# Expert tiles of a routed FFN: 28 tiles of 256 rows, then units of 128 rows, with the short chunk of the hidden dimension first

## The reference

```python
x = x + _L0_xattn_ref(_layernorm(x, axis=-1), ctx_1024, ctx_1024, w_proj, b_proj)
x = x + _L0_ffn_ref(_layernorm(x, axis=-1), Wg, W1, W2, W3)

def _L0_ffn_ref(x, Wg, W1, W2, W3):          # 8 experts, hidden 682
    gate_logits = jnp.einsum('bsd,ed->bse', x, Wg)
    top_v, top_i = jax.lax.top_k(gate_logits, 2)
    ...
    gating = jax.nn.softmax(sparse_logits, axis=-1)
    h1 = jnp.einsum('bsd,ehd->bseh', x, W1)
    h2 = jnp.einsum('bsd,ehd->bseh', x, W2)
    hidden = jax.nn.silu(h1) * h2
    expert_out = jnp.einsum('bseh,edh->bsed', hidden, W3)
    return jnp.einsum('bsed,bse->bsd', expert_out, gating)
```

## Time and profile before

| | us |
|---|---|
| median of 3 runs | 873.97 |
| lowest, highest | 872.97, 878.98 |
| the profiled execution, its own time | 874.99 |
| its span, first to last instruction | 873.1 |

### The profile page before, as it was taken

The page is one execution under the profiler, slowest core; times in us unless marked ns, Lnnn a source line. Parts: engine busy times, 40 slices in busy tenths (PEclk is TensorE's granted clock), DMA queues, the critical chain, the costliest instruction groups (busy, mean ns, idle before and its releaser), DMA issues.

```text
span 873.1 us, 20010 instructions
## 1 busy us (share of the span) xinstructions
PE 784.8 (90%) x6472; PEld 481.2 (55%) x6472; DVE 602.1 (69%) x1224; ACT 557.6 (64%) x970; POOL 439.6 (50%) x431
## 2 busy tenths in 40 slices
PE   0578898989989899897989899999999999999995
PEld 0112233333333333332326788888888888888884
DVE  4888888979888898899924557555555555555553
ACT  3369789888897988966884454444444444444442
POOL 4555435786777868675643665222224222222222
PEclk9999999999999999999999999999999999999998
DMA  8575756866659685674266699999997699383832
GB/s 184 179 191 167 202 124 225 188 217 157 189 209 188 215 170 190 182 161 169 106 195 225 190 252 299 293 308 271 267 261 160 161 250 255 57 251 49 250 41 25
DMA packets 105959, 167.57 MB, mean 192 GB/s; under 512 B 54688, under 2 KB 83232, under 8 KB 101280
## 3 DMA queue, kind: packets, MB, share of 16 engines
q1 hardware_dynamic: 92448, 148.76, 60.0%
q0 software_dynamic: 13440, 17.90, 10.6%
HBM read 119.75 MB, written 42.55 MB: 186 GB/s over the span
## 4 chain that ended last, share of the span: by engine, by line
PE 48%; ACT 2%; issue 1%; POOL 1%; DMA 0%; DVE 0%; POOLq 0%; ACTq 0%; DVEq 0%
PE ps L1376 10%; PE ps L1378 10%; PE ps L1380 10%; PE ps L1394 4%; PE ps L1396 4%; PE ps L1398 4%; PE ps L1299 2%; ACT probs L842 1%; PE ps L1403 1%; PE ps L1284 1%; POOL slots L474 1%; ACT z_n L847 1%; PE ps L1327 0%; PE ps L1338 0%; PE ps L1271 0%
## 5 line engine op out<-in xcount | busy, mean ns | idle before, releaser
L973 DVE TENSOR_REDUCE neg_max<-ps 128x2 f16<-128x1024 f32 x256 | 309.1, 1221 | 37.6 <-PE ps L1271 32.9
L842 ACT ACTIVATE probs<-ps 128x1024 f32<-128x1024 f32 x256 | 259.0, 1024 | 61.7 <-PE ps L1284 61.2
L769 POOL DMA_INDIRECT out<-y,aim x72 | 113.4, 1574 | 237.6 <-DVE y L1202 160.0
L1376 PE MATMUL ps<-zt,w 128*128 128x256 f16 x792 | 216.0, 273 | 1.4 <-issue 1.3
L1378 PE MATMUL ps<-zt,w 128*128 128x256 f16 x792 | 215.9, 273 | 0.0
L1380 PE MATMUL ps<-zt,w 128*128 128x256 f16 x792 | 215.9, 273 | 0.0
L876 ACT ACTIVATE silu<-ps 128x256 f32<-128x256 f32 x216 | 82.7, 383 | 183.4 <-PE ps L1380 173.8
L1183 DVE SCALAR_TENSOR_TENSOR hid<-ps,silu 128x256 f32<-128x256 f32 x216 | 91.7, 425 | 136.0 <-ACT silu L876 128.3
L1299 PE MATMUL ps<-probs,v_ext 128*32 128x512 f32 x1024 | 138.7, 613 | 5.3 <-ACT heads L910 4.4
L1271 PE MATMUL ps<-k_stack,q_stack 48*128 48x512 f16 x512 | 104.3, 406 | 35.4 <-ACT probs L842 17.8
L1284 PE MATMUL ps<-q_stack,k_stack 49*128 49x512 f16 x512 | 101.9, 396 | 7.3 <-DVE neg_max L973 7.1
(11 more groups left out here) (126 smaller groups left out, 908.0 us busy)
## 6 DMA issues: line engine op xcount, KB each, us to landing
w<-w_parts SPq DMA_DIRECT2D x36, 1408.0 KB
w<-w_parts SPq DMA_DIRECT2D x36, 768.0 KB
w_in<-in_w SPq DMA_DIRECT2D x16, 704.0 KB, 6.0
v_ext<-in_v SPq DMA_DIRECT2D x8, 1024.0 KB, 5.6
k_stack<-k SPq DMA_DIRECT2D x48, 128.0 KB, 5.3
q_stack<-qt SPq DMA_DIRECT2D x48, 128.0 KB, 5.0
w_in<-in_w SPq DMA_DIRECT2D x8, 768.0 KB, 5.0
w_parts<-w_hi SPq DMA_DIRECT2D x16, 352.0 KB, 2.3
```

What stands on the lines that cost most here:

```text
L769: nc.gpsimd.indirect_dma_start(out=out, out_offset=bass.IndirectOffsetOnAxis(ap=aim[frm][:, t, 0:1].bitcast(U32), axis=0), in_=y[frm][:, t ...
L842: nc.scalar.activation(probs[g % 2][:, j:j + 2, k, :], pair_banks[PLACE["exp", u] % 3], ACT.Exp, scale=0.25).then_inc(s_exp, 1)
L973: nc.vector.tensor_reduce(neg_max[b % 2][:, i, c:c + 3:2], pair_banks[PLACE["max", u] % 3], AX.X, ALU.max, negate=True).then_inc(s_red, 1)
L1376: nc.tensor.matmul(dst, w[:, kk, 1, cols], z16[:, kk, :], start=(kk == 0), stop=False)
```

## The change

The 8192 rows are cut otherwise: `FULL_TILES` = 28 tiles of 256 rows, which any routing can fill by more than half, then units of 128 rows, of which `FIRM_UNITS` - 28 = 8 always exist and up to 7 more are behind a comparison. The units are straight code (15 copies on each engine) where before there was a loop of two tiles and one copy. A unit loads 128 rows, its matmuls of the up phase have 128 columns, its down phase has 16 matmuls, its ACT and DVE instructions are 128 wide, and it has one add. In each tile and unit the tail becomes the first chunk of the up phase, and the last but one of the down phase. `table` now runs three times: for tiles 0 to 11, for 12 to 27, and for the units; the third pass runs on DVE in four steps behind each of the tiles 6 to 11. SP waits for the second table before tile 12 and reads the number of units before it issues the first unit's loads. The zero rows are 128 per expert. Core of the diff:

```diff
-FIRM_TILES = 2 * TOKENS // SLOTS
-FFN_TILES = FIRM_TILES + E - 1
+FULL_TILES = (2 * TOKENS - E * P) // SLOTS
+FIRM_UNITS = FULL_TILES + 2 * TOKENS // P - SUB * FULL_TILES
+FFN_UNITS = FULL_TILES + (2 * TOKENS + E * (P - 1)) // P - SUB * FULL_TILES
+CHUNKS = (FULL,) + tuple(range(FULL))
...
+def subs(least):
+    return SUB if least < FULL_TILES else 1
+def subs_ahead(k):
+    return k * SUB if not isinstance(k, int) or k <= FULL_TILES else k + FULL_TILES * (SUB - 1)
...
+def last_units(eng, total, *steps):
+    for k in range(FIRM_UNITS, FFN_UNITS):
+        with eng.If(total > k):
+            for step in steps:
+                step(k, k // 2, k % 2, k)
...
-                rows = z_dram[bass.ds(first, SLOTS), :]
-                sp.dma_start_transpose(zt16[par][:, :, :], rows[:, 0:W].bitcast(F16)).then_inc(f_z[par], 16)
+                n = subs(least)
+                rows = z_dram[bass.ds(first, n * P), :]
+                sp.dma_start_transpose(zt16[par][:, :, 0:n * P], rows[:, 0:W].bitcast(F16)).then_inc(f_z[par], 16)
...
-                    sp.dma_start(z_dram[bass.ds(first, SLOTS), :].rearrange("(s p) c -> p s c", p=P),
-                                 fill[:, :, :]).then_inc(f_pad, 16)
+                    sp.dma_start(z_dram[bass.ds(first, P), :], fill[:, 0, :]).then_inc(f_pad, 16)
...
-            total = tiles_in_use(sp)
+            sp.wait_ge(s_tab, K_FULL_TAB)
...
-            firm_tiles(sp, KNOWN, FIRM_TILES, (load_rows, 0), (load_up, 0), (load_down, 0))
-            last_tiles(sp, total, (load_rows, 0), (load_up, 0), (load_down, 0))
+            firm_units(sp, KNOWN, FULL_TILES, load_rows, load_up, load_down)
+            total = tiles_in_use(sp)
+            known_tiles(FULL_TILES, FIRM_UNITS, load_rows, load_up, load_down)
+            last_units(sp, total, load_rows, load_up, load_down)
...
-                pool.wait_ge(f_y, k * SUB + (t + 1))
+                pool.wait_ge(f_y, subs_ahead(k) + (t + 1))
                 if least and t == 0:
-                    pool.wait_ge(f_add, k * (SUB * 16))
+                    pool.wait_ge(f_add, subs_ahead(k) * 16)
...
-                        nc.scalar.activation(silu[m % 2][to, :], ps[rows, bank, 0:W], ACT.Silu,
+                        nc.scalar.activation(silu[j % 2][to, 0:n], ps[rows, bank, 0:n], ACT.Silu,
...
-                if least >= FIRM_TILES:
-                    dve.wait_ge(f_add, (k - 1) * 32)
-                elif least >= KNOWN:
-                    dve.wait_ge(f_add, (k - TURNS + 1) * 32)
+                if least >= KNOWN:
+                    dve.wait_ge(f_add, subs_ahead(k - TURNS + 1) * 16)
...
-                        if least >= 1 and m == FULL % 2:
-                            dve.wait_ge(f_tail, k * 2)
+                        if j == 2:
+                            dve.wait_ge(f_tail, (k + 1) * 2)
...
+            tables.append(table(2))
+            next(tables[0])
+            def late_table_steps(k, half, par, least):
+                for _ in range(4):
+                    table_step()
+            known_tiles(EARLY, KNOWN, whole(tile), late_table_steps)
...
-                for m in range(HC):
-                    u, bank = k * HC + m, (m + 2 * par) % 4
+                for j in range(HC):
+                    u, m, bank = k * HC + j, CHUNKS[j], (j + 2 * par) % 4
...
-                            nc.tensor.matmul(dst, w[:, kk, 1, cols], z16[:, kk, :],
+                            nc.tensor.matmul(dst, w[:, kk, 1, cols], z16[:, kk, 0:n],
...
-                for m in range(HC):
-                    pe.wait_ge(f_lo, k * HC + (m + 1))
-                    for t in range(SUB):
+                for m in (*range(FULL - 1), FULL, FULL - 1):
+                    pe.wait_ge(f_lo, k * HC + (CHUNKS.index(m) + 1))
+                    if m == FULL:
+                        pe.wait_ge(f_tail, (k + 1) * 2)
+                    for t in range(subs(least)):
```

More of the change, by code:

```diff
@@ L55 @@
 NCNT = TOKENS // SLOTS
[L56 to L58 removed]
+C_PCNT = C_CNT + NCNT
+C_K = C_PCNT + NCNT
+C_KS = C_K + LIST
+C_KP = C_KS + LIST
+C_E = C_KP + LIST
 C_EPS = C_E + E
@@ L222, in known_tiles, with firm_units @@
             step(k, k // 2, k % 2, k)
-def firm_tiles(eng, first, end, *steps):
+def subs(least):
+    return SUB if least < FULL_TILES else 1
+def subs_ahead(k):
+    return k * SUB if not isinstance(k, int) or k <= FULL_TILES else k + FULL_TILES * (SUB - 1)
+def firm_units(eng, first, end, *steps):
     with eng.Fori(0, (end - first) // TURNS) as i:
         for turn in range(TURNS):
-            for step, _ in steps:
+            for step in steps:
                 step(i * TURNS + (first + turn), i * (TURNS // 2) + (first + turn) // 2, turn % 2, first + turn)
[L233 to L243, removed]
+def last_units(eng, total, *steps):
+    for k in range(FIRM_UNITS, FFN_UNITS):
+        with eng.If(total > k):
+            for step in steps:
+                step(k, k // 2, k % 2, k)
 def ge(eng, sem, value):
@@ L1079, in small_step, with table @@
                     slots_and_gate(b)
-            def table(early):
+            def table(part):
                 def step(ins):
@@ L1086, in step @@
                     ins.then_inc(s_tab, 1)
+                early, late = part == 0, part == 2
+                first, end = ((0, KNOWN), (KNOWN, FULL_TILES), (FULL_TILES, FFN_UNITS))[part]
+                rows, c_cnt, c_rows = (P, C_PCNT, C_KP) if late else (SLOTS, C_CNT, C_KS)
+                some, n = slice(first, end), end - first
                 reg = con[:, C_REG:C_REG + E]
[L1089 to L1092, removed]
+                tt, stt = nc.vector.tensor_tensor, nc.vector.scalar_tensor_tensor
+                counts = con[:, c_cnt:c_cnt + NCNT].unsqueeze(1).broadcast_to([P, E, NCNT])
                 big = [P, n, E]
@@ L1096, in table @@
                     yield
[L1097 to L1101, removed]
+                    step(stt(out=cnt[:, :], in0=run[:, :], scalar=-float(SLOTS), in1=reg,
+                             op0=ALU.add, op1=ALU.subtract))
+                elif not late:
                     yield
@@ L1120, in table @@
                 yield
-                step(nc.vector.scalar_tensor_tensor(out=origin[:, :], in0=t_begin[:, :], scalar=-float(SLOTS),
-                                                    in1=reg if early else used[:, :], op0=ALU.mult, op1=ALU.add))
+                step(stt(out=origin[:, :], in0=t_begin[:, :], scalar=-float(rows),
+                         in1=reg if early else used[:, :], op0=ALU.mult, op1=ALU.add))
                 yield
@@ L1142, in table @@
                 step(nc.vector.tensor_scalar(row_tab[:, some], row_f[:, some], float(E * REGION), None, ALU.add))
-                if not early:
+                if late:
                     yield
@@ L1181, in tile @@
                         rows = slice(0, P) if m < FULL else upper
[L1182 removed]
+                        gated = ps[:, bank, W:W + n] if m < FULL else ps[upper, bank, 0:n]
                         nc.vector.scalar_tensor_tensor(
[L1184 to L1187 removed]
+                            out=hid[j % 2][rows, 0:n], in0=gated, scalar=1.0 / WSCALE,
+                            in1=silu[j % 2][rows, 0:n], op0=ALU.mult, op1=ALU.mult).then_inc(f_hid, 1)
@@ L1238, in _ @@
                     if b in (EARLY_BATCHES - 1, B - 1):
-                        tables.append(table(b < B - 1))
+                        tables.append(table(0 if b < B - 1 else 1))
                         next(tables[0])
```

175 lines of the change are left out of this document (94 added, 81 removed).

## The result

The changed kernel takes 872.1 us (median of 20 runs), the kernel before 876.63 (20 runs beside it): a ratio of 0.9946, 95% interval 0.993 to 0.9962. By that ratio it is 4.7 us faster, 3.3 to 6.1, and within 1%. Forecast were 868.0 with a range of 859 to 880, and a change of -5.9. Of the 4.1 us between 872.1 and 868.0, 2.7 lie in the kernel before: the forecast started from 873.97, the median of 3 runs, and that of 20 is 876.63.

A forecast was written before the change was run, and what follows sets the result against it. PE was taken as the bound from about 500 us. Its stretch goes from 87.4 to 83.4 (81.6 units, 1.8 reading), the end loses 1.86: -5.9, so 874.99 becomes 869.1; the median lies 1.0 lower, 868, range 859 to 880.

The forecast's parts named there:

- Unit without loads: 128-row unit that nothing else holds: 6.3 us, with last down matmuls waiting for ACT and DVE; bounds 5.5 and 7.0.
- rival C: Up phase of the units: pitch 0.083 instead of 0.057, a unit 7.8 us; +6.1, 880 us; chance 0.05.
- Units with loads: Four units after unit 28: paced by DMA time of new weights, 7.8 us each, 31.2 together; bounds 6.3 and 8.5.
- rival E: Units with new weights: idle PE lowers the clock, costing about 4 us per such unit; slower; chance 0.06.
- Reading the number of units: Before the conditional units: reading the count and the comparisons cost 1.8 us, as before the change.
- The tail, first: Full tiles: 26 down matmuls (2.84 us) cover the 2.52 until lo; slack 0.3, no cost on 28 tiles.
- The end: After the last matmul: the last unit has one add instead of two, 1.86 us less.
- Rival D: POOL's adds in the units become the bound, each waiting for the previous landing of 7.7; +12, 886 us; chance 0.08.
- Rival A: Units: weight loads stay hidden, twelve units of 6.3 us; -11.9, 862 us; chance 0.15.
- rival B: Units: small ACT and DVE steps don't shrink and loads come late, 7.0 and 8.5 us; +2.5, 876; chance 0.20.
- SP does not bind: SP's queue in the units: its issues and table reads take 6.4 us per unit, so it does not set the pace.

The follow-up runs named there:

- changed_again: The changed kernel run once more without an edit; 871.4 us, ratio 0.9932 to the kernel before.
- units_no_loads: The changed kernel with the new-weights flag 0 for all units, so none loads weights; 863.34 us, ratio 0.9861 to the kernel before.
- both_ends_weights_first: The changed kernel with units taken from both list ends in turn and SP issuing w12 before the rows; 865.25 us, ratio 0.9872 to the kernel before.
- weights_first: The changed kernel with SP reading tables ahead of the wait and issuing w12 before rows, targets and w3; 870.11 us, ratio 0.992 to the kernel before.

## Why the prediction was right, and where its steps were not

The number and the place were right: units without loads close to the forecast length, and four to five units lengthened by loads. Step by step, from the start of unit 28 to the last matmul (82.0, forecast 83.4 to that matmul's slot):

- **Unit without loads**: 6.12, forecast 6.3. The up phase is 66 matmuls in 3.69, a pitch of 0.056 as read off; rival C's 0.083 falls. The last three down matmuls begin 2.09 after the up phase (859.95 to 862.04 in the last unit), where the sum of ACT and DVE steps said 2.2. Twelve units: -2.2. The Trainium skill (TensorE: Matmul & The Clock Gate, section Back-to-back issue gap) has about 81 ns per matmul for such a stream; the trace does not agree, with 56 ns and a weight load to each matmul.
- **Units with loads**: 32.1 for four, forecast 31.2; with the shorter base it is the larger miss. Taken apart: each unit that is followed by a gap is 0.16 longer beside it (the gap counts from the end of the last matmul, not from its slot), so the waits for loads cost (0.18 + 2.38 + 0.39 + 2.29) + 4 x 0.16 = 5.9; forecast were 4 x 1.5 = 6.0. The gaps stand one unit earlier than forecast (ahead of units 29 to 32, not 30 to 33), and two are large and two small. What was not in the sum is the clock, which was forecast at 1.00 throughout: units 30 and 32 are 1.0 longer each by the lower level, 2.1 together. That is rival E in part: its mechanism took place, at 1.0 per unit instead of 4, since the lower level lasted for part of an up phase only. The up phase was 1.6 longer (5.3 against 3.69), and of that 1.0 is left at the unit's end. How the loads' cost is shared out is not the same in each execution: in changed_again the waits take 6.85 + 5 x 0.16 = 7.65, and the clock 1.0 in one unit. So that the waits of the first profile meet the forecast 6.0 so closely is luck in part. That the clock's falls belong to the gaps is shown by units_no_loads and both_ends_weights_first, 1.00 in the same stretch.
- **Reading the number of units**: 0.75, forecast 1.8; -1.05. The forecast kept it as it was. order_only, whose only edit is the order of the chunks, has 0.70, so, by one profile each, the order made it smaller; how is not shown.
- **The tail, first**: "no cost on 28 tiles" holds but for tile 4, which is 1.3 longer (1.55 in order_only). It lies ahead of unit 28 and is met by the 0.7 that the turns of the loop lack.
- **The end**: from the last matmul's start to the end of the span, 9.43 against 10.69 before, so -1.26 instead of -1.86. The add is issued 1.8 sooner after PE, as forecast, but from it to the end are 7.74 instead of 7.19.

POOL's timeline, two adds between the loads and two of the last (in brackets the idle time and what ended it):

```profile
792.76 1.56 POOL L783 DMA_INDIRECT out<-y,aim  x1 [7.49 <-DMA out<-y,aim]
802.04 1.56 POOL L783 DMA_INDIRECT out<-y,aim  x1 [7.73 <-DMA out<-y,aim]
...
851.73 1.56 POOL L783 DMA_INDIRECT out<-y,aim  x1 [4.55 <-DVE y L1224]
...
863.96 1.56 POOL L783 DMA_INDIRECT out<-y,aim  x1 [3.81 <-DVE y L1224]
```

- **Rival D** (adds): they trailed, 4.7 to 9.3 apart while weights loaded, five of them issued as the one before landed, but from 826 on all but one wait for `y`, that is for PE (the one at 858.60 is put down to issue). The landing fell to about 4 as the loads ended, as the earlier trace rows said, and the lag was made up. In both_ends_weights_first, whose loads end later, it was not. **Rival A** (hidden loads) and **rival B** did not come; units_no_loads has what A would have given: -12.2 by its ratio, where A said -11.9.

**The step that was right in its number and incomplete in its reason** is "SP does not bind: 6.4 per unit". That is SP's rate. A load also has a way: 3.7 from the free buffer to its issue, 7 to 9 until its unit starts. A buffer is used every second unit, so a loop of buffer free, load, up phase takes 11.4 + 3.7 = 15.1 (unit 28's up phase ends at 783.94, unit 30 starts at 795.38) to 16.4 for two units: 7.6 to 8.2 per unit, the same as the 7.8 of DMA time. Two limits of one size stood beside each other, and the prediction saw one. Spreading the loads alone left the way, and for more units (875.01); shortening the way alone left the DMA work (870.11); both together (865.25) took 5.9 of the 8.1 us that the loads cost on PE from unit 28 to the last matmul (82.0 in the changed kernel, 76.1 with both, 73.9 without loads).

The sum: -2.2 for the units, +2.0 for the loads (clock), -1.05 for the reading, so -1.25 on PE's stretch; +0.6 at the end. Each of the four is a miss, and that they add up to no more than -0.65 is luck. The late part is -6.6 where -5.9 was forecast, and -5.6 in changed_again; the medians give -4.7 [-6.1, -3.3] and, in the second set of runs, -6.0 [-7.7, -4.1].

What is open: why the lower clock in the attention, which every kernel here has near 400 us, lasts longer in some executions; why tile 4 waits for DVE with the tail first; and the last gap of 1.19.

## What to carry to other kernels

When a tile is halved, what its weights cost is not, and the time that hid them is: work out both the DMA time per tile and the whole way of one load (buffer free, the issuing queue's own steps, landing) against the time in which a buffer must turn round, since either alone can set the pace, and mending one shows little, or makes it worse, while the other is as long. Gaps on PE can be paid for twice, by the clock behind them. Before a difference of two profiled executions is explained, measure the stretch that was changed by itself: here the rest of the kernel moved by 5 us in one of them.

## What the runs showed of the hardware

- In the stretch of the units, the longer gaps on PE were followed by a fall of the granted clock to its lower level and the shorter were not, in every run here. In the 5 us from the end of gaps of 1.98, 2.10, 2.27, 2.29 (in two runs), 2.38, 2.52 and 3.56 the clock was 0.66 to 0.69; after 0.98, 1.19, 1.29 (in two runs), 1.30, 1.36, 1.40, 1.49, 1.76 and 1.84 it was 1.00. In the attention, where PE has many small gaps, have it at 0.50 behind one of 1.49.
- A conditional load of 1408 KB, with 768 KB behind it, had its unit start 8.6 after its issue while the DMA queues were otherwise little used, and 12.4 in a row of such loads (787.30 to 799.72 in weights_first, where the wait that ended last was for its rows).
- Matmuls of 128 columns with a 128x128 weight load each run at 0.056 us in a stream of 66, half of the 0.109 of 256 columns.
